# Lag transforms on sums and differences of lags, and a reordered start, in an autocorrelation attention plus low-rank FFN kernel

## The reference

```python
x = x + autocorrelation(layernorm(x), ctx, ctx)
x = x + ffn(layernorm(x))
# autocorrelation, per batch and column, L = 512:
corr = ifft(fft(q) * conj(fft(k))).real
w, idx = top_k(corr, int(2 * log(L)))            # 12 lags
w = softmax(w)
out[pos] = sum_i w[i] * v[min(idx[i] + pos, L - 1)]
# ffn:
out = x @ W.T + bias + sum_e coeffs[e] * scales[e] * (x @ A[e].T) @ Bf[e].T
```

## Time and profile before

| | us |
|---|---|
| median of 3 runs | 2713.62 (2708.38 to 2715.58) |
| the profiled execution's own time | 2710.2 |
| its span, first to last instruction | 2708.4 |
| TensorE busy | 2599.7 (96%) |
| GpSimd busy | 2156.1 (80%) |
| VectorE busy | 1820.4 (67%) |
| ScalarE busy | 1009.2 (37%) |

### The profile page before, as it was taken

How to read it: one execution, slowest core, us unless ns; L and a number is a source line. 1 busy time by engine, 2 the same in 40 slices (tenths; PEclk the granted TensorE clock), 3 DMA queues, 4 the chain that set the end, 5 groups by cost and what they waited for, 6 DMA issues and landing times.

```text
span 2708.4 us, 38028 instructions
## 1 busy us (share of the span) xinstructions
PE 2599.7 (96%) x13312; PEld 1658.5 (61%) x13312; DVE 1820.4 (67%) x4710; ACT 1009.2 (37%) x1778; POOL 2156.1 (80%) x1558
## 2 busy tenths in 40 slices
PE   4999967899999999999999999999999999999999
PEld 3666655566666666666666666666666666654444
DVE  6888879667776677667776677667775677544100
ACT  4788746433344234433344234433332233201000
POOL 5799999788997899888997899878897899655222
PEclk8999988999999999999999999999999999999999
DMA  8399998956786687957796678956775587858953
GB/s 319 102 257 276 268 245 184 267 160 235 246 263 198 201 261 254 267 163 230 249 263 198 201 257 258 267 162 229 245 229 170 203 259 230 201 181 300 272 172 116
DMA packets 550031, 613.41 MB, mean 226 GB/s; under 512 B 322640, under 2 KB 448720, under 8 KB 532176
## 3 DMA queue, kind: packets, MB, share of 16 engines
q1 hardware_dynamic: 549840, 610.99, 75.0%
HBM read 383.35 MB, written 151.00 MB: 197 GB/s over the span
## 4 chain that ended last, share of the span: by engine, by line
PE 79%; POOL 10%; DMA 4%; DVE 3%; issue 2%; SPq 2%; ACT 0%; POOLq 0%; DVEq 0%; ACTq 0%
PE f_ps L814 15%; PE f_ps L816 15%; PE f_ps L818 15%; PE a_ps L740 10%; PE a_ps L698 10%; PE a_ps L779 6%; PE a_ps L794 3%; PE a_ps L795 3%; POOL p_lo L1174 2%; POOL a_zu L1081 1%; POOL a_zv L1081 1%; POOL f_x1p L1081 1%; DMA p_hi_t<-p_hi 1%; POOL a_rows L1081 1%; POOL a_zf L1081 1%
## 5 line engine op out<-in xcount | busy, mean ns | idle before, releaser
L814 PE MATMUL f_ps<-f_whi,f_hhi 128*128 128x512 f16 x2048 | 776.9, 379 | 6.6 <-issue 2.8
L816 PE MATMUL f_ps<-f_wlo,f_hhi 128*128 128x512 f16 x2048 | 776.9, 379 | 0.0
L818 PE MATMUL f_ps<-f_whi,f_hlo 128*128 128x512 f16 x2048 | 776.7, 379 | 0.0
L898 ACT ACTIVATE a_side<-a_ps 128x256 f32<-128x256 f32 (+1 forms) x192 | 87.0, 454 | 1043.2 <-PE a_ps L779 808.0
L740 PE MATMUL a_ps<-a_w_lag,lags 128*128 128x256 f16 x3072 | 356.8, 273 | 2.2 <-DMA a_w_lag<-a_w_row 1.3
L818 PEld LDWEIGHTS f_ps<-f_whi,f_hlo 128*128 128x128 f16 x2048 | 200.6, 98 | 242.0 <-issue 0.8
L816 PEld LDWEIGHTS f_ps<-f_wlo,f_hhi 128*128 128x128 f16 x2048 | 200.5, 98 | 230.5 <-issue 0.6
L740 PEld LDWEIGHTS a_ps<-a_w_lag,lags 128*128 128x128 f16 x3072 | 300.8, 98 | 62.0 <-issue 5.1
L814 PEld LDWEIGHTS f_ps<-f_whi,f_hhi 128*128 128x128 f16 x2048 | 200.5, 98 | 221.3 <-issue 7.2
L1081 POOL TENSOR_TENSOR a_prod<-a_prod,a_tf 128x512 f32<-128x512 f32 x128 | 160.4, 1276 | 166.1 <-DVE a_tf L1208 166.1
L1081 POOL TENSOR_TENSOR a_zv<-a_zv,a_tw 128x512 f32<-128x512 f32 x128 | 183.2, 1450 | 122.7 <-DVE a_tf L1208 122.6
(11 more groups left out here) (133 smaller groups left out, 4993.7 us busy)
## 6 DMA issues: line engine op xcount, KB each, us to landing
f_whi<-whi_scratch SPq DMA_DIRECT2D x128, 512.0 KB, 4.8
f_wlo<-wlo_scratch SPq DMA_DIRECT2D x128, 512.0 KB, 5.6
a_rows<-in_x_dram SPq DMA_DIRECT2D x62, 1024.0 KB, 8.5
vs<-in_ctx_dram SPq DMA_DIRECT2D x64, 512.0 KB, 6.3
xs<-in_x_dram SPq DMA_DIRECT2D x64, 512.0 KB, 6.9
parts_scratch<-a_so SPq DMA_DIRECT2D x64, 512.0 KB, 6.9
x_scratch<-a_rows SPq DMA_DIRECT2D x32, 1024.0 KB, 5.1
f_x1p<-x_scratch SPq DMA_DIRECT2D x32, 1024.0 KB, 6.8
```

The lines of the kernel that those rows point to most:

```text
L814: nc.tensor.matmul(f_ps[:, t, :], h_hi[q][:, kq, rows_t], w_hi[u % WR][:, :, kq, :], start=(k == 0), stop=False)
L816: nc.tensor.matmul(f_ps[:, t, :], h_hi[q][:, kq, rows_t], w_lo[u % WR][:, :, kq, :], start=False, stop=False)
L818: mm = nc.tensor.matmul(f_ps[:, t, :], h_lo[q][:, kq, rows_t], w_hi[u % WR][:, :, kq, :], start=False, stop=(k == DB - 1))
L898: return nc.scalar.activation(out, source, ACT.Copy, **how)
```

## The change

The gather's transform needs cosines and sines at all 256 lags of a half. Cosines are even and sines odd about lag 128, up to a sign that depends on the frequency's parity, so weights at n and 256 - n can be summed and subtracted first, and each matrix then needs only one 128-lag half. The order of lags inside `corr` is rearranged (in the constant `inv`) so that n and 256 - n stand in the same place of two blocks. VectorE makes the difference and the sum in place in PSUM (`lags_folded`), for which ScalarE first copies one block of each half to `a_side` (`copy_far`). `scale` and `weights_low` now wait for `lags_folded`; `copy_output`, which reuses `a_side`, waits for it too. Lags 0 and 128 have no partner and get an extra small matrix in two of the four sets.

Two more edits: the first root's helpers `veps` and `sq` are moved from SBUF to PSUM (`f_ps`) and two multiplications change places; `add_products(0)` stands ahead of `fold_values(1)` on GpSimd.

```diff
     lags = np.stack([np.cos(np.outer(sums_at, cyc)), np.sin(np.outer(parts_at, cyc)),
                      np.cos(np.outer(parts_at, neg)), np.sin(np.outer(sums_at, neg)),
                      np.zeros((T, T)), np.zeros((T, T))])
...
@@ inverse_root
-        nc.vector.tensor_tensor(sq, root, root, ALU.mult).then_inc(link, 1)
+        nc.vector.tensor_tensor(sq, root, veps, ALU.mult).then_inc(link, 1)
         dve.wait_ge(link, at + 2)
-        nc.vector.tensor_tensor(sq, sq, veps, ALU.mult).then_inc(link, 1)
+        nc.vector.tensor_tensor(sq, sq, root, ALU.mult).then_inc(link, 1)
@@ lags
+                sums, differences = 2 * h, 2 * h + 1
                 for k in range(2):
                     for cls in range(2):
-                        for j in range(2):
-                            for constant, part in ((0, 0), (0, 1), (1, 0)):
-                                mm = nc.tensor.matmul(ps[:, pair + k, cls, :], lag_mat[:, constant, j, 2 * cls + k, :],
-                                                      w_lag[:, part, 2 * h + j::TB, :],
+                        main = sums if cls == k else differences
+                        out = ps[:, pair + k, cls, :]
+                        extra = cls == 0
+                        for constant, part in ((0, 0), (0, 1), (1, 0)):
+                            mm = nc.tensor.matmul(out, lag_mat[:, constant, 2 * cls + k, :], w_lag[:, part, main::TB, :],
+                                                  start=(constant + part == 0), stop=(constant == 1 and not extra))
+                        if extra:
+                            other = differences if k == 0 else sums
+                            for part in range(2):
+                                mm = nc.tensor.matmul(out, lag_mat[:, 0, 4 + k, :], w_lag[:, part, other::TB, :],
+                                                      start=False, stop=(part == 1))
@@ ScalarE
+            def copy_far(n):
+                for g in range(SUB):
+                    act.wait_ge(kept, SUB * n + g + 1)
+                    copy(side[:, g, :].rearrange("p (h l) -> p h l", h=2), lags_of(corr[:, g, :])[:, :, 1, :]
+                         ).then_inc(far_copied, 1)
@@ scale
                     act.wait_ge(share_known, SUB * n + g + 1)
+                    act.wait_ge(lags_folded, SUB * n + g + 1)
@@ copy_output
-                act.wait_ge(corr_folded, SUB * min(n + 2, N))
+                act.wait_ge(lags_folded, SUB * min(n + 2, N))
@@ ScalarE's window, behind move_upper(w + 1)
                 if w < N:
+                    copy_far(w)
                     scale(w)
@@ GpSimd's start
             fold_values(0)
             fold_queries(0)
+            add_products(0)
             fold_values(1)
-            add_products(0)
             fold_queries(1)
@@ VectorE's choose, at its end
+                for g in range(SUB):
+                    dve.wait_ge(far_copied, SUB * n + g + 1)
+                    by_lag, copied = lags_of(corr[:, g, :]), side[:, g, :].rearrange("p (h l) -> p h l", h=2)
+                    near, far = by_lag[:, :, 0, 1:T], by_lag[:, :, 1, 1:T]
+                    nc.vector.tensor_tensor(far, near, copied[:, :, 1:T], ALU.subtract)
+                    nc.vector.tensor_tensor(near, near, copied[:, :, 1:T], ALU.add).then_inc(lags_folded, 1)
@@ weights_low
                     dve.wait_ge(scaled, SUB * n + g + 1)
+                    dve.wait_ge(lags_folded, SUB * n + g + 1)
@@ first_gain
+                veps, sq = f_ps[:, 0, 0:TB], f_ps[:, 1, 0:TB]
```

More of the change, by code:

```diff
@@ L69, in position_order, with lag_order @@
     return np.concatenate([p, 2 * T - 1 - p, 2 * T + p, L - 1 - p])
+def lag_order():
+    n = np.arange(1, T)
+    return np.concatenate([[T], n, [0], 2 * T - n])
 def transform_matrices():
     half = 2 * T
-    at, lag = np.arange(T) + 0.5, np.arange(half)
+    at, lag = np.arange(T) + 0.5, lag_order()
     even, odd = np.arange(0, T, 2), np.arange(1, T, 2)
@@ L83, in transform_matrices @@
     fold[1][:, 0] = nyquist
-    lags = np.stack([np.cos(np.outer(lag, cyc)), np.sin(np.outer(lag, cyc)),
-                     np.cos(np.outer(lag, neg)), np.sin(np.outer(lag, neg))])
-    lags[1][:, 0] = -np.cos(np.pi * lag)
-    lags = lags.reshape(4, 2, T, T).transpose(2, 1, 0, 3)
+    near = lag[T:].copy()
+    near[1:] = lag[1:T]
+    sums_at, parts_at = lag[:T], near
+    lags = np.stack([np.cos(np.outer(sums_at, cyc)), np.sin(np.outer(parts_at, cyc)),
+                     np.cos(np.outer(parts_at, neg)), np.sin(np.outer(sums_at, neg)),
+                     np.zeros((T, T)), np.zeros((T, T))])
+    lags[1][:, 0] = 0
+    lags[1][0, 0] = -1
+    lags[4][0, :] = 1
+    lags[5][:, 0] = -np.cos(np.pi * sums_at)
+    lags = lags.transpose(1, 0, 2)
     high = lags.astype(np.float16)
@@ L100, in transform_matrices, with lags_of @@
             "out": out.transpose(1, 0, 2), "ident": np.eye(T), "ident16": np.eye(T).astype(np.float16)}
+def lags_of(weights):
+    return weights.rearrange("p (h a l) -> p h a l", h=2, a=2)
 def at_least(engine, sem, value):
@@ L164, in __init__ @@
         self.fold = sb("fold", [T, 4, T])
-        self.lags = sb("lags", [T, 2, 2, 4, T], F16)
+        self.lags = sb("lags", [T, 2, 6, T], F16)
         self.inv = sb("inv", [T, 2, 2, 2 * T])
@@ L265, in flow @@
         row_sums, minus_mean, squares = (sb(f"a_{name}", [T, 2 * TB]) for name in ("row_sums", "minus_mean", "squares"))
-        veps, root, sq = (sb(f"a_{name}", [T, TB]) for name in ("veps", "root", "sq"))
+        root = sb("a_root", [T, TB])
         s_veps, s_root, s_sq = (sb(f"a_s_{name}", [T, 1]) for name in ("veps", "root", "sq"))
@@ L330, in flow @@
         kept = sem("a_kept")
+        far_copied = sem("a_far_copied")
+        lags_folded = sem("a_lags_folded")
         share_known = sem("a_share_known")
@@ L734, in lags @@
             def lags(pair, h, mm_done):
+                sums, differences = 2 * h, 2 * h + 1
                 for k in range(2):
                     for cls in range(2):
-                        for j in range(2):
-                            for constant, part in ((0, 0), (0, 1), (1, 0)):
-                                mm = nc.tensor.matmul(ps[:, pair + k, cls, :], lag_mat[:, constant, j, 2 * cls + k, :],
-                                                      w_lag[:, part, 2 * h + j::TB, :],
-                                                      start=(j == 0 and constant + part == 0),
-                                                      stop=(j == 1 and constant == 1))
+                        main = sums if cls == k else differences
[9 more added lines that the diff above has]
+                                                      start=False, stop=(part == 1))
                     mm.then_inc(mm_done, 1)
@@ L1375, in first_gain @@
                 dve.wait_ge(x_mv_done, 1)
-                nc.vector.tensor_scalar(veps[:, :], x_mv[:, :, 1], EPS, None, ALU.add).then_inc(x_var_done, 1)
+                veps, sq = f_ps[:, 0, 0:TB], f_ps[:, 1, 0:TB]
+                nc.vector.tensor_scalar(veps, x_mv[:, :, 1], EPS, None, ALU.add).then_inc(x_var_done, 1)
                 dve.wait_ge(x_var_done, 1)
-                inverse_root(nc, dve, veps[:, :], root[:, :], sq[:, :], stat[:, 0, 0, :], 1.0, x_link, 0
+                inverse_root(nc, dve, veps, root[:, :], sq, stat[:, 0, 0, :], 1.0, x_link, 0
                              ).then_inc(x_link, 1)
```

## The result

| | before | after |
|---|---|---|
| median time, us | 2712.13 (2708.38 to 2715.58) | 2646.35 (2639.25 to 2652.75) |
| profiled execution, us (span) | 2710.2 (2708.4) | 2646.18 (2644.4) |
| window 1 starts | 62.81 | 61.00 |
| window 2 | 96.54 | 93.65 |
| window 14 | 495.07 | 498.92 |

The ratio is 0.9757, 95% interval 0.9728 to 0.9786: 2.4% faster, where 2643 us were forecast.

The account below looks back on a forecast made before the run. TensorE was taken to bound windows 1, 2 and 14 to 63, GpSimd to pace 3 to 8. Terms -88.9 + 0.9 + 17.3 + 3 - 3.7 - 1.1 + 2 = -70.5 gave 2639.7; 3.4 for the median made 2643 us, range 2618 to 2669.

Parts of the forecast that it names:

- The lag matmuls, -88.9: Windows 14 to 63 and window 64's last lag pair: 16 fewer matmuls per window save 1.74 us each, 88.9 us.
- Late weights: Windows 19, 27, 35, 43, 51, 59: TensorE waits 3.1 us each for turned weights; 18.6 us, net +17.3.
- the 3 us two windows later: Two windows after each late row window (36, 20, ...), GpSimd is again later against TensorE: 0.5 us each for six.
- The landing: Turned weights for window 35 land 75.75 us after window 33's start, while wanted at 72.6.
- Rival 2: No late weights, as GpSimd makes up time or transposes behind the row's store get quicker: 2623 us, chance 0.19.
- the estimate from the rate in the Trainium skill: Window 34's two transposes, at 261 GB/s plus about 2 us fixed, done 4 us after issue, so no wait.
- rival 3: Other row windows' weights late too (18 windows x 1.0), windows 2 to 13 +8: 2669 us, chance 0.27.
- rival 4: Weights turned late in each of the 50 windows, making the kernel slower than before: 2759 us, chance 0.02.
- The start, -3.7: Before window 1: helpers in PSUM and earlier first correlation gain 4.6, less 0.85 for the weights' longer way.
- Window 1 itself: Window 1, set by TensorE: 1.74 saved, less 0.85 and 0.2 given back at the queries; -1.1 us taken.
- Windows 2 to 13, +2.0: VectorE's round grows 0.85 but disappears where DMA or GpSimd held it: +2.0 us in all, bounds -2 and +10.
- The sign I named for this: A window 14 starting later than 495 would show that windows 2 to 13 were misjudged.

Follow-up runs that it names:

- the start edits alone: Kernel before, with only the root's helpers moved to PSUM and `add_products(0)` put ahead of `fold_values(1)`: 2709.6 us, ratio 0.9995.
- the lag change alone: Changed kernel with the helpers' move to PSUM and the reordering of `add_products(0)` undone: 2648.1 us, ratio 0.9766.
- the last row early: Changed kernel with the copy of chunk 2's last values row issued right behind the second x chunk: 2645.4 us, ratio 0.9759.
- no early folds: Changed kernel with ScalarE's copies and VectorE's folds of the lags left out for chunks 0 to 13: 2643.9 us, ratio 0.9751.
- a quarter: One of four 512-column operations replacing VectorE's low-row subtraction, in the kernel with transposes ahead of row store and load in both row windows: 2680.2 us.

## Why the prediction was right

**The lag matmuls, -88.9: right.** 0.109 us each and 36.30 us per window, against 36.31.

**Late weights, right in mechanism and place.** The waits came at windows 19, 27, 35, 43, 51 and 59: 3.01, 3.97, 2.69, 2.60, 2.67 and 1.40, together 16.3 where 18.6 were forecast. For the 3 us two windows later there are 0.51, 0.53 and 0.35 behind windows 20, 52 and 60, and 0.32 behind window 35. The landing was forecast 75.75 us behind window 33's start and came at about 75.4. Rival 2 fails on the 6.6 to 8.0 us of the landing, and with it the estimate from the rate in the Trainium skill, page "DMA: Bandwidth & Descriptors", section "Latency and other measured facts"; of rival 3's other row windows only 35 was late, by those 0.32; rival 4 had no sign. What the sum did not have is the clock: 1.69 us each in windows 19 and 27, and 1.7 in window 14, 5.1 in all. The waits, on the other hand, cost 16.7 us more than before where the sum had 20.3. From window 14 to window 63 the change brought 61.9 us where the sum had 64.1, so two errors largely cancel there, which is luck.

**The start, -3.7: too large.** I let VectorE's old row of waits bound it, and didn't look at what else ScalarE would wait for once it came early. The first correlation moved by 3.51 us (39.56 to 36.05). Steps of the root that took 1.12 to 1.26 us in SBUF, others there being at 0.16, now all take 0.16 to 0.17:

```profile
16.71 0.17 DVE L142 TENSOR_TENSOR f_ps<-a_root,f_ps 128x4 f32<-128x4 f32 x1
...
36.05 0.51 PE L805 MATMUL a_ps<-inv,a_prod 128*128 128x256 f32 x1
```

But `last` held ScalarE for 5.14, and window 1 starts only 1.81 earlier; with that row early it starts 5.1 earlier than before. The sum also carried the -3.7 through to the end, and the start edits alone show nothing of their 2.59 left at window 14. Window 1 itself gave 1.08, as forecast (1.1).

**Windows 2 to 13, +2.0: too small.** They took 6.7 more. Two steps failed. That a longer round of VectorE's would mostly vanish behind GpSimd and the transfers: the lag change alone costs these windows 3.8, and leaving out folds and copies gave back 5.75 us over windows 1 to 13. And that they leave a gain at the start alone: the start edits by themselves cost them 2.8. My upper bound of 10 covered it. The sign I named for this, window 14 later than 495, is there: 498.92.

**Why the sum held.** The largest term, the lag matmuls, was right, and the rest are small beside it. Against its own profiled execution it was 6.5 us short (2639.7 against 2646.2): 6.6 by window 14, 2.2 more up to window 63, less 2.5 behind that, where profiled executions scatter. The 3.4 that I added for the median hid half of it, by luck: the changed kernel's profiled execution was no faster than its median.

VectorE is busy 81 us more (forecast 90), ScalarE 47 (forecast 50).

## What to carry to other kernels

When the bounding engine gets faster, write down for every loop beside it how late its result lands and when it is wanted: the margins say where and how much is lost, and at window 35 they did to 0.4 us. Then look what stands in the queue ahead of the late transfer; moving a load that nobody wants yet behind it was worth 17 us, more than all edits at the start. A gain in a stage that another engine or the transfers pace need not reach the end: 2.6 us at the start were gone by window 14. And a reordered queue moves other engines' operations against each other, so read the durations of the neighbours again after it.

## What the runs showed of the hardware

**TensorE's clock after a wait.** Behind the wait of 3.01 us at window 19, the granted clock (third column from the right) averages 0.67, 0.50 and 0.98 in three stretches of 2 us. So it is at 0.50, the lower of its two levels, 1.2 GHz, in part of them, and window 19 is 1.69 us longer than 36.30. Behind 2.69 us at window 35 it stays at 2.4:

```profile
687.58:689.58 2.00, 2.00 (x13) 1.56 (x14) 0.61 (x2) 2.00 (x4) 2.00 (x3) 0.67 0.94 344
689.58:691.58 2.00, 2.00 (x8) 1.00 (x7) 1.64 (x4) 0.59 (x2) 1.78 (x2) 0.50 0.97 310
691.58:693.58 2.00, 2.00 (x10) 0.89 (x9) 0.33 (x1) 0.00 (x0) 1.59 (x2) 0.98 0.83 249
```
```profile
1279.62:1281.62 2.00, 2.00 (x18) 1.70 (x19) 0.85 (x2) 2.00 (x4) 2.00 (x3) 1.00 0.94 340
```

The length of the wait alone doesn't tell. With the last row early the clock stayed up behind a wait of 3.24 us, and with no early folds it fell behind one of 2.79. In the lag change alone it fell behind one of 2.68, and in window 14 of the changed kernel behind one of 2.14, where the kernel before waited 2.44 and kept it.

**Small operations beside GpSimd.** Some 128x4 steps of the root take 1.12 to 1.26 us with their tiles in SBUF while GpSimd adds, and all take 0.17 with the helpers in PSUM. The first, compared above, then has one input and its output there.

**An operation held for 11 to 14 us**, with two inputs in SBUF, while nine of GpSimd's additions pass, as above: 13.06 us instead of 2.28, and 14.9 instead of 0.68 for a quarter.
